# Four attention blocks in one program: score products on 32-row groups of fp32 projections instead of stacks of high and low parts moved by DMA

## The reference, cut to what matters

```python
# L0: 4 heads of 4 channels; softmax over n (the query index)
q = Wq @ x + bq; k = Wk @ x + bk; v = Wv @ x + bv
A = softmax(q^T k, axis=n); x = x + gamma * (Wo @ (v A) + bo)
# L1: one head of 16 channels for q and k, 128 for v; softmax over keys
x = x + gamma * (v @ softmax(q^T k)^T)
# L2: 8 heads of 16; q from group_norm(x), k and v from group_norm(2x2-pooled x): 256 keys
x = x + wproj @ (softmax(q^T k / 4) v)
# L3: one head of 128 channels, group_norm with 32 groups
x = x + out_w @ (softmax(q^T k / sqrt(128)) v) + out_b
```

## Time and profile before

| | us |
|---|---|
| median of 3 timed runs | 430.88 |
| span of the profiled execution | 430.1 |
| TensorE matmuls busy | 366.4 (85%) |
| VectorE busy | 250.3 (58%) |
| ScalarE busy | 184.1 (43%) |
| SyncE and hardware queues: DMA share of 16 engines | 15.9% |

### The profile page before, as it was taken

How to read it: one execution, slowest core, us unless ns; L and a number is a source line. 1 busy time by engine, 2 the same in 40 slices (tenths; PEclk the granted TensorE clock), 3 DMA queues, 4 the chain that set the end, 5 groups by cost and what they waited for, 6 DMA issues and landing times.

```text
span 430.1 us, 4516 instructions
## 1 busy us (share of the span) xinstructions
PE 366.4 (85%) x1712; PEld 210.2 (49%) x1712; DVE 250.3 (58%) x325; ACT 184.1 (43%) x218; POOL 70.9 (16%) x43
## 2 busy tenths in 40 slices
PE   3378999999999998819899997969198898999994
PEld 1245444445545562315654653556165366567652
DVE  4296775557775776108887355981099036591723
ACT  2013468775574347801466525245005821613110
POOL 9920000000004600000000054003300002201910
PEclk9995999999999998977999999989689999999998
DMA  7321000000200000693020000005950000000011
GB/s 264 52 37 12 2 1 3 1 3 0 51 1 0 2 0 7 82 122 42 5 52 2 1 0 2 0 6 71 117 59 4 5 0 2 0 1 2 1 49 49
DMA packets 4644, 11.91 MB, mean 28 GB/s; under 512 B 668, under 2 KB 2268, under 8 KB 4496
## 3 DMA queue, kind: packets, MB, share of 16 engines
q1 hardware_dynamic: 4624, 11.64, 15.9%
HBM read 2.81 MB, written 1.05 MB: 9 GB/s over the span
## 4 chain that ended last, share of the span: by engine, by line
PE 68%; DVE 12%; issue 7%; DMA 6%; ACT 5%; SPq 0%; ACTq 0%; DVEq 0%
PE attn_acc L900 12%; PE products L879 12%; PE attn_acc L895 10%; PE products L842 7%; PE products L861 5%; DVE neg_max L655 5%; PE products L916 4%; PE products L836 3%; ACT probs L542 3%; PE products L802 3%; DMA score_ops<-max_rows 2%; DMA score_ops<-stage_lo 2%; PE products L806 2%; PE products L924 2%; PE products L829 2%
## 5 line engine op out<-in xcount | busy, mean ns | idle before, releaser
L542 ACT ACTIVATE probs<-products 128x1024 f32<-128x1024 f32 x128 | 127.2, 1027 | 96.7 <-PE products L879 65.8
L655 DVE TENSOR_REDUCE neg_max<-products 128x1 f32<-128x1024 f32 x96 | 114.2, 1221 | 50.1 <-PE products L842 47.5
L879 PE MATMUL products<-score_ops 128*128 128x512 f32 x224 | 78.2, 445 | 6.6 <-DMA score_ops<-max_rows 3.0
L842 PE MATMUL products<-score_ops 128*128 128x512 f32 x160 | 58.5, 462 | 12.3 <-DMA score_ops<-stage_lo 8.8
L900 PE MATMUL attn_acc<-probs,v 128*128 128x512 f32 x128 | 63.0, 603 | 0.0
L651 DVE TENSOR_REDUCE neg_max<-products 128x4 f32<-128x1024 f32 x32 | 37.5, 1219 | 36.6 <-PE products L836 36.5
L879 PEld LDWEIGHTS products<-score_ops 128*128 128x128 f32 x224 | 38.6, 193 | 40.9 <-DVE neg_max L655 12.6
L381 POOL TENSOR_TENSOR prob_sum<-probs 128x1024 f32<-128x1024 f32 x4 | 9.5, 2372 | 265.4 <-ACT probs L542 239.4
L895 PE MATMUL attn_acc<-probs,v 128*32 128x512 f32 x384 | 51.7, 624 | 0.5 <-ACT probs L542 0.4
L381 POOL TENSOR_TENSOR prob_sum<-prob_sum,probs 128x1024 f32<-128x1024 f32 x16 | 38.4, 2400 | 72.8 <-ACT probs L542 71.3
L842 PEld LDWEIGHTS products<-score_ops 128*128 128x128 f32 x160 | 29.7, 205 | 36.9 <-DVE neg_max L655 11.3
(11 more groups left out here) (116 smaller groups left out, 314.9 us busy)
## 6 DMA issues: line engine op xcount, KB each, us to landing
score_ops<-stage_lo SPq DMA_DIRECT2D x16, 256.0 KB, 14.3
score_ops<-stage_hi SPq DMA_DIRECT2D x8, 256.0 KB, 13.0
w<-w_rest SPq DMA_DIRECT2D x1, 1124.0 KB, 7.4
x<-x SPq DMA_DIRECT2D x2, 512.0 KB, 4.7
y<-x SPq DMA_DIRECT2D x2, 512.0 KB, 2.6
tmp<-row_selector SPq DMA_DIRECT2D x1, 512.0 KB, 8.2
score_ops<-stage_k_hi SPq DMA_DIRECT2D x4, 128.0 KB
score_ops<-stage_k_lo SPq DMA_DIRECT2D x4, 128.0 KB
```

Of the source, the lines that this page charges most:

```text
L542: nc.scalar.activation(P[:, n % NP, :], slot(s), ACT.Exp, scale=SCALE[L]).then_inc(read_act, 1)
L655: nc.vector.tensor_reduce(out=NM[:, u % 2, t:t + 1], in_=slot(s), op=ALU.max, axis=AX.X, negate=True).then_inc(read_dve, 1)
L842: mm = nc.tensor.matmul(slot(s)[:, h], ST[b][0:KROWS, ks, 128 * t:128 * (t + 1)], ST[b][0:KROWS, rs, h], start=True, stop=True)
L879: mm = nc.tensor.matmul(slot(s)[:, h], red, ST[b][0:KROWS, ks, h], start=True, stop=True)
```

## The change

The stacks, their staging tiles and their DMAs are gone. Weights are laid out on the host so that a projection puts each head (layers 0 and 2), or each of four copies (layer 1), on a 32-row group of partitions: rows 32j to 32j+31. There are more projections for this: k and q apart in layers 0 and 1, q in two parts and k twice as wide in layer 2. ScalarE writes a float32r copy (RA, RB, KR2) and VectorE an fp32 copy (FA, FB, KF2); in layer 0 only the rounded pair is kept, with high and low parts beside each other inside the 32 rows. Every `A` and `B` product of layers 0 to 2 contracts over 32 rows, and two of them on different row groups fill the two halves of a tile. `B` of layers 1 to 3 multiplies fp32 operands. The maxima go by DMA into row 16 of each group: 2 DMAs per `top` in layer 0, 4 in layers 1 and 2 and 1 in layer 3, where it was 1 everywhere. The split of the maxima into two parts goes. In layer 0 a unit is half the columns of two heads instead of one head. `den` writes four 32-column groups, and `dsum` is gone.

```diff
 elif kind == "A":
     g, t = s[3], s[4]
     if t == 0:
-        pe.wait_ge(stacks_in[b], stacks_count(L, b))
...
+        wait_read(pe, ("q", L, b))
+        wait_read(pe, ("k", L, b))
+    if L == 0:
+        mh, (mt, nh) = g % 2, divmod(t, 2)
+        for a in range(2):
+            rows = slice(GROUP * (2 * (g // 2) + a), GROUP * (2 * (g // 2) + a) + GROUP)
+            tile = slice(HALF * mh + 128 * mt, HALF * mh + 128 * (mt + 1))
+            mm = nc.tensor.matmul(slot(s)[:, halves[a]], RA[b][rows, tile], RB[b][rows, halves[nh]],
+                                  start=True, stop=True)
-        for h in halves:
-            mm = nc.tensor.matmul(slot(s)[:, h], ST[b][0:KROWS, ks, 128 * t:128 * (t + 1)],
-                                  ST[b][0:KROWS, rs, h], start=True, stop=True)
...
 elif kind == "B":
...
+    elif L == 2:
+        half, kt, hp = t // 4, t // 2 % 2, t % 2
+        for a in range(2):
+            rows = slice(GROUP * (2 * hp + a), GROUP * (2 * hp + a) + GROUP)
+            mm = nc.tensor.matmul(slot(s)[:, halves[a]], KF2[b][rows, g, 128 * kt:128 * (kt + 1)],
+                                  (FA, FB)[g][b][rows, halves[half]], start=True, stop=True)
+    else:
+        for h in halves:
+            nc.tensor.matmul(slot(s)[:, h], FB[b][:, 128 * t:128 * (t + 1)], FA[b][:, h],
+                             start=True, stop=False)
-        for i, (r, k) in enumerate(((8, 0), (8, 1), (9, 0), (9, 1))):
-            for h in halves:
-                nc.tensor.matmul(slot(s)[:, h], ST[b][:, r, tile], ST[b][:, k, h],
-                                 start=i == 0, stop=False)
...
 elif kind == "top":          # SyncE
-    sp.dma_start(S[MAXROW:MAXROW + 2, k0:k0 + kn, :], ZR[0:16 * kn, i, :]).then_inc(maxrows_in[b], 16)
+    elif L == 2:
+        for j in range(4):
+            row = GROUP * j + ONE
+            sp.dma_start((FA, FB)[g][b][row:row + 1, :], ZR[8 * j:8 * j + 8, i, :]).then_inc(maxrows_in[b], 16)
...
 elif kind == "den":
-    for t in range(NT):
-        mm = nc.tensor.matmul(slot(s)[0:64, 0:128], sel[:, 28 - 4 * t:92 - 4 * t],
-                              src[:, 128 * t:128 * (t + 1)], start=t == 0, stop=t == NT - 1)
+    for i, (src, sel) in enumerate(parts):
+        for half in range(2):
+            for j in range(4):
+                t = 2 * j + half
+                mm = nc.tensor.matmul(slot(s)[32 * j:32 * j + 32, 0:128],
+                                      sel[:, 4 - 4 * half:36 - 4 * half], src[:, 128 * t:128 * (t + 1)],
+                                      start=i == 0 and half == 0, stop=i == len(parts) - 1 and half == 1)
```

More of the change, by code:

```diff
@@ L117, in epilogue @@
     if L == 0:
[L118 removed]
+        return [("y", L, b), ("den", L, b, g), ("bcast", L, b, g)]
     if L == 2 and g == 1:
@@ L205, in attention_layers @@
     for s in plan:
-        if s[0] in ("PV4", "PV1") and s[5] == 1:
+        if s[0] == "PV4" or s[0] == "PV1" and s[5] == 1:
             n += 1
-            for t in range(4 * s[4], 4 * s[4] + 4) if s[0] == "PV4" else [s[4]]:
+            for t in (2 * s[4], 2 * s[4] + 1) if s[0] == "PV4" else [s[4]]:
                 pv_done_at[("B", *s[1:4], t)] = n
@@ L353, in wait_sum_free @@
         def wait_sum_free(eng, s):
-            p = [p for p in plan[:plan.index(s)] if p[0] == "den" and p[1] != 2]
+            p = [p for p in plan[:plan.index(s)] if p[0] == "den" and p[1] in (1, 3)]
             if p:
@@ L546, in _ @@
                     act.wait_ge(pv_done, pv_done_at[("B", *u, TILES[u][-1])])
-                    last = o_last.get(o_before[u])
-                    if last and last[0] == "y":
+                    last = o_last.get(o_before.get(u))
+                    if last and last[0] in ("y", "den"):
                         wait_tile(act, last)
@@ new lines, in _ @@
+                        for i in range(2):
+                            for a in range(2):
+                                rows = slice(GROUP * (2 * hp + a), GROUP * (2 * hp + a) + GROUP)
+                                tile = slice(128 * (2 * qp + i), 128 * (2 * qp + i + 1))
+                                mm = nc.tensor.matmul(slot(s)[:, HALF * a + NKV * i:HALF * a + NKV * (i + 1)],
+                                                      (RA, RB)[g][b][rows, tile], KR2[b][rows, g, :],
+                                                      start=True, stop=True)
+                    else:
+                        for h in halves:
+                            mm = nc.tensor.matmul(slot(s)[:, h], RA[b][:, 128 * t:128 * (t + 1)], RB[b][:, h],
+                                                  start=True, stop=True)
@@ L853, in _ @@
+                    full(s, nc.tensor.transpose(slot(s)[0:z.shape[1], 0:128], z, w("ident")))
                 elif kind == "B":
@@ L888, in _ @@
                         wait_read(pe, ("v", L, b))
                     if kind == "PV4":
[L891 to L896 removed]
+                        tiles = [("B", L, b, g, 2 * t0 + i) for i in range(2)]
@@ new lines, in _ @@
+                        wait_read(pe, tiles[1])
+                        h = halves[g % 2] if L == 0 else halves[t0 // 2]
+                        for i, q in enumerate(tiles):
+                            for a in range(2):
+                                j = 2 * i + a
+                                lhs = V0[b][:, 2 * (g // 2) + a, 2 * t0 + i, :] if L == 0 else V2[b][:, g, t0 % 2, j, :]
+                                mm = nc.tensor.matmul(acc[32 * j:32 * j + 32, h], lhs, P[:, b_no[q] % NP, halves[a]],
+                                                      start=t0 == 0 if L == 0 else t0 % 2 == 0,
+                                                      stop=t0 == 3 if L == 0 else t0 % 2 == 1)
@@ L926, in _ @@
                     full(s, mm)
-                elif kind == "dsum":
-                    pe.wait_ge(w2_in, 16)
-                    pe.wait_ge(acc_out, out_no[("out", 0, b, 3)] + 1)
-                    for h in halves:
-                        for i in range(H0):
-                            mm = nc.tensor.matmul(slot(s)[32 * i:32 * i + 32, h], w("den0"), O[o_tile[(0, b, i)]][:, h],
-                                                  start=True, stop=True)
-                    full(s, mm)
                 elif kind == "y" and L == 0:
```

519 lines of the change are left out of this document (237 added, 282 removed), and 6 rows, old and new, of the table REST.

## The result

The changed kernel takes 433.55 us (median of 17 runs, 432.03 to 435.67), the kernel before on the same chip 431.41 (17 runs). The ratio is 1.0042, 95% interval 1.0021 to 1.0062: slightly slower, where 398 us was forecast. The profiled execution has a span of 431.2 us against 430.1.

What follows compares the result with a forecast made beforehand. The path was taken as TensorE's stream plus some 27 us of stacks and 10 of maxima. Terms -27 - 4 + 13 - 19 + 10 - 2 - 15 + 5 + 6 = -33 gave 398 us, range 378 to 416.

Steps and rivals of the forecast that it cites:

- item 2: The low clock behind the long stops before layer 2 goes with them: -4 us (0 to -6).
- the rival that it stays low: In layer 0 TensorE idles in VectorE's shade and its clock stays at 1.2 GHz: 438 us; chance 0.04.
- The sign that I had named: A granted clock near 1.0 where layer 2 starts on either image would show the forecast right.
- Item 1: Waits for stacks at the start, layer 1 of image 0 and layer 2 of either image go: -27 us.
- Item 3: More projections, the first at half speed at the program's start, five more and two wider k: +13 us.
- Item 4: Layer 0: tiles as row-group pairs at 0.24 us save 2.4 us per unit, eight units: -19 us (-14 to -23).
- Item 5: Layers 1 and 2: 48 A tiles cheaper (-11), 48 B tiles now fp32 at 0.93 us (+22): +10 us.
- Item 6: Layer 3: eight float32r products, 1.84 us, become two fp32 products, 1.72 us, in 16 tiles: -2 us.
- Item 7: Each `den` of 1.89 us gets cheaper with four column groups at once, and layer 0's `dsum` goes: -15 us.
- Item 8: More DMAs of maxima, 0.61 us of SyncE each, complete rows later, mostly felt in layer 2: +5 us (+2 to +10).
- Item 9: Array shape changes rise from 125 to some 195, 0.16 us each, layer 0's hidden by VectorE: +6 us (0 to +17).
- the third rival: Changing the array's shape costs 0.33 us each, 23 us instead of 6 in all: 415 us; chance 0.17.

Runs made afterwards that it cites:

- the strided one: Changed kernel, whole result, maxima of a top in one DMA writing rows 32 apart in layers 0 and 2, layer 1 keeping four: 426.3 us, ratio 0.986.
- both causes made smaller: Changed kernel with pairs of products on 64 rows each and one DMA of maxima per top: 414.57 us, ratio 0.959 to the kernel before.
- the mirror test: Kernel before with its A and B products of layers 0 to 2 over 32 rows instead of 128: 534.79 us, ratio 1.243.

## Why the prediction was wrong

**The step that failed** is the clock: item 2, which had the low clock go with the stops (-4 us), and the chance of 0.04 given to the rival that it stays low. Measured is +38 us lost to it. The argument against the rival, "at half speed TensorE would be busy all the time again, and busy stretches have the full clock", took the busy share for what the clock answers to. In the rows I had both went together, and the busy stretches of the kernel before had all products on 128 rows; no row spoke of 32. The sign that I had named, a granted clock near 1.0 where layer 2 starts, reads 0.50 (199 to 215.5 us). The rival too was drawn too narrow: it had the clock down for all of layer 0 and nowhere else. It falls where the other kernels lose it as well, behind stops and thin stretches, and stays down longer, at 157 us four times as long.

- **Item 1** (-27): the stops went. The first exponential starts at 32.7 us instead of 36.7, and layer 2 has no DMA before its A tiles. Right, though idle time fell by only 8 us in all.
- **Item 3** (+13): the projections' records (L756, L760) fill 40 us against 18, +23. 23 of the 40 are at half clock; counted at full clock they are +13. The count was right, the speed not.
- **Item 4** (-19): near at full clock. From one unit's first PV4 to the next's it is 9.5 and 8.2 us (59.8, 69.3, 77.5), where it was 11.5 and 10.3: 2 us less per unit, 2.4 taken. What limits it was read wrongly: VectorE is busy for 66% there, ScalarE for 89%.
- **Item 5**: what fp32 costs over float32r in these tiles, 33 us by its prices, measured as 22 on 64 rows. Its +22, against the old stacks, was not measured by itself. A float32r pair alone between two PV4 takes 0.43, which is the 0.24 with a change of shape on either side; within a run of pairs one follows the next after 0.23 (63.41 to 63.65).
- **Item 6**: eight float32r products against two fp32 ones per tile, 1.84 and 1.72 us, as forecast.
- **Item 7** (-15): `den` and `dsum` took 22 us of TensorE before (L916 and L933), `den` takes 7 now. Right.
- **Item 8** (+5): 11 by the run with one DMA, 7 by the strided one. Each DMA holds SyncE for 0.63 us as forecast, and with one DMA idle time fell by 5; the rest came through the clock.
- **Item 9** (+6): nearly right in its price. The chain in layer 1, first before, then after:

```profile
135.38 1.72 PE attn_acc L900 x4
137.09 0.46 PE products L879 x2
```

```profile
139.82 1.92 PE attn_acc L869 x4
141.73 0.43 PE products L784 x2
142.16 1.06 PE attn_acc L869 x2
```

The PV1 takes 0.20 more and the pair 0.19 more than the 0.24 forecast for it: 0.2 per change, where 0.16 was taken and the third rival wanted 0.33. By the matmul records the shape changes 67 times more (116 to 183), 70 were counted.

The sum without the clock holds in the main. With both causes made smaller (414.57 us) work at full clock and idle time together fell by 26 us (12 and 14) against the kernel before; the items other than the clock give 34, without item 8, whose DMAs this version doesn't have. Of the 17 us by which it still lies above 398, 13 are the clock: 9 more lost where 4 were to be won. The 8 that the items had too many are not taken apart; pairs on 64 rows, which can't run two at once, are one reason. Open is what the clock's rule is; the runs show only what moves it.

## What to carry to other kernels

A busy share of TensorE is not the array's work. Before cutting the rows that a product uses, or mixing shapes of products one by one, ask what part of the array will move in the stretches behind stops, and price the stream there at half clock. Zeros on the idle rows, to fill 64 instead of 32, cost 16 us of work here and gave 22 us of clock back; with fewer DMAs the version came out 15 us faster. Read the granted clock beside the busy share, by stretch, and check it by the durations of a known instruction.

## What the runs showed of the hardware

- TensorE stayed at half clock for 126 us on end while its records called it 100% busy (the products of zeros over 128 rows, 30.2 to 156.4 us, in the 527.63 us execution).
- Four 32-row products of two pairs start within 10 ns (75.234 to 75.244 us) if they lie on four row groups, and within 20 ns in fp32 (237.284 to 237.304 us). On the same groups the next pair comes mostly 0.33 us later, 0.41 in one case; on 64-row halves 0.23 to 0.34.
- Single products of 32 rows behind each other on one group cost the same as products of 128 rows: at full clock a first step of 0.34 us and then 0.23, at half clock 0.43 (the mirror test).
- Changing the array's shape costs about 0.2 us at full clock (layer 1) and 0.29 at half clock (the products of zeros over 128 rows), and the records call that time busy.
- One DMA that writes four rows 32 partitions apart replaces four at 0.63 us of SyncE each.
